# Row means of tiles 10 to 15: by two GpSimd transfers each through a row in memory instead of a TensorE transpose

## What is computed

```python
xn = _layernorm(x, axis=-1)                      # (x - mean) * rstd, per row
q = xn @ Wq.T + bq                               # every 4th head of 32 is used: 8 heads x 128
sig_q = elu(q) + 1
retrieved = (sig_q @ M) / (sig_q . z + 1e-6)     # per head
attention = repeat(retrieved, 4 heads) @ Wo.T
dense = xn @ (w * w_scale) + b
out = x + attention + dense
```

## Time and profile before

| | us |
|---|---|
| median of 3 runs | 237.94 |
| the runs | 237.94, 237.75, 238.29 |
| the profiled execution, its own time | 237.95 |
| its span, first to last instruction | 236.1 |
| TensorE busy in it | 232.5 |
| VectorE busy | 174.0 |
| ScalarE busy | 125.2 |
| GpSimd busy | 107.4 |

### The profile page before, as it was taken

The page is one execution under the profiler, slowest core; times in us unless marked ns, Lnnn a source line. Parts: engine busy times, 40 slices in busy tenths (PEclk is TensorE's granted clock), DMA queues, the critical chain, the costliest instruction groups (busy, mean ns, idle before and its releaser), DMA issues.

```text
span 236.1 us, 3421 instructions
## 1 busy us (share of the span) xinstructions
PE 232.5 (98%) x1037; PEld 188.4 (80%) x1037; DVE 174.0 (74%) x275; ACT 125.2 (53%) x285; POOL 107.4 (45%) x117
## 2 busy tenths in 40 slices
PE   8999999999999999999999999999999999999995
PEld 3688788888888788888888888888888888888895
DVE  2989999897589987997858859585667879362511
ACT  4845358687298386585547253654637445630300
POOL 1029437856932356558350442524045598480000
PEclk9999999999999999999999999999999999999999
DMA  6999999999590144471727272431134456879521
GB/s 227 389 412 414 356 250 254 224 212 218 133 278 17 41 95 130 96 180 48 175 89 178 72 196 77 91 104 39 52 94 97 136 135 159 191 189 182 193 98 44
DMA packets 24081, 38.76 MB, mean 164 GB/s; under 512 B 5440, under 2 KB 13248, under 8 KB 22912
## 3 DMA queue, kind: packets, MB, share of 16 engines
q1 hardware_dynamic: 18816, 26.10, 33.7%
q0 software_dynamic: 3808, 11.14, 24.5%
q10 hardware_dynamic: 1440, 1.31, 1.9%
HBM read 25.95 MB, written 4.19 MB: 128 GB/s over the span
## 4 chain that ended last, share of the span: by engine, by line
PE 98%; DVE 0%; issue 0%
PE attn_ps L876 14%; PE attn_ps L878 14%; PE attn_ps L877 13%; PE q_ps L876 10%; PE q_ps L878 10%; PE q_ps L877 10%; PE dense_ps L876 6%; PE dense_ps L878 6%; PE dense_ps L877 6%; PE dense_ps L967 2%; PE q_ps L916 1%; PE q_ps L904 1%; PE q_ps L911 1%; PE attn_ps L916 1%; PE attn_ps L904 1%; PE attn_ps L911 1%
## 5 line engine op out<-in xcount | busy, mean ns | idle before, releaser
L489 ACT ACTIVATE s<-s,rden 128x128 f32<-128x128 f32 x128 | 39.2, 390 | 39.3 <-DVE rden L707 37.6
L341 POOL TENSOR_TENSOR e_and_sz<-s,z_b 128x512 f32<-128x512 f32 x32 | 41.7, 1340 | 39.6 <-DVE den L703 39.6
L876 PE MATMUL attn_ps<-P_hi,aT_hi 128*128 128x512 f32 (+1 forms) x136 | 53.0, 389 | 0.0
L878 PE MATMUL attn_ps<-P_hi,aT_lo 128*128 128x512 f32 (+1 forms) x136 | 52.2, 384 | 0.0
L877 PE MATMUL attn_ps<-P_lo,aT_hi 128*128 128x512 f32 (+1 forms) x136 | 52.1, 383 | 0.0
L876 PE MATMUL q_ps<-WqT_hi,xT_hi 128*128 128x512 f32 x104 | 40.7, 391 | 0.0
L878 PE MATMUL q_ps<-WqT_hi,xT_lo 128*128 128x512 f32 x104 | 40.5, 389 | 0.0
L877 PE MATMUL q_ps<-WqT_lo,xT_hi 128*128 128x512 f32 x104 | 40.5, 389 | 0.0
L691 DVE SCALAR_TENSOR_TENSOR q_ps<-q_ps,rstd,bq_b 128x512 f32<-128x512 f32 x28 | 21.0, 752 | 17.6 <-PE q_ps L878 17.6
L876 PEld LDWEIGHTS attn_ps<-P_hi,aT_hi 128*128 128x128 f32 x136 | 25.6, 188 | 6.1 <-issue 0.6
L878 PEld LDWEIGHTS attn_ps<-P_hi,aT_lo 128*128 128x128 f32 x136 | 25.6, 188 | 5.2
(11 more groups left out here) (96 smaller groups left out, 356.1 us busy)
## 6 DMA issues: line engine op xcount, KB each, us to landing
x<-in_WoT POOLq DMA_DIRECT2D x6, 1024.0 KB, 11.0
x<-in_b POOLq DMA_DIRECT2D x16, 256.0 KB, 4.4
out<-x SPq DMA_DIRECT2D x15, 256.0 KB, 2.4
x<-in_x SPq DMA_DIRECT2D x14, 256.0 KB, 3.6
xT<-in_xT SPq DMA_DIRECT2D x13, 256.0 KB, 3.8
aT<-s SPq DMA_DIRECT2D x104, 32.0 KB, 2.3
MT<-s SPq DMA_DIRECT2D x72, 32.0 KB, 1.9
x<-in_WoT SPq DMA_DIRECT2D x2, 1024.0 KB, 13.3
```

The lines of the kernel that those rows point to most:

```text
L341: nc.gpsimd.tensor_tensor(sz_eps[:, :, h * D // 2:(h + 1) * D // 2].rearrange("p g (j c) -> p j g c", j=2), by_quarter(sbuf_s[:, t % SRING ...
L489: last = nc.scalar.activation(a_g, a_g, ACT.Copy, scale=rden[:, t % 2, g:g + 1])
L876: nc.tensor.matmul(out, x_hi, w_hi, start=start, stop=False)
L878: return nc.tensor.matmul(out, x_lo, w_hi, start=False, stop=stop)
```

## The change

Means of tiles 2 to 9 stay with TensorE. For tiles 10 to 15 the transpose (L886) and the copy from its bank (L430) are gone, six of each. In their place GpSimd issues two transfers per tile. `send_mean(t)` writes the column of 128 means, 4 bytes from each partition, to row t of a table in memory, once VectorE has them. `bring_mean(t)` waits until that has landed, and reads the row back to all 128 partitions (512 bytes each) into `mean_b`. `center(t)` waits for this second landing in place of ScalarE's copy. It stands one step later than before: tile t + 1 in step t, behind the first tile of `times_z`, where it was tile t + 2 at the end of step t.

```diff
--- before.py
+++ after.py
@@ -35,6 +35,7 @@
     XRING = 4
     HRING = 4
     BEHIND = 3
+    FIRST_CARRIED = 10
     assert P == D and HID == 512 and HALF == 512 and R == 4 and T == 16 and G == 8 and K == 4
 
     with ExitStack() as ctx:
@@ -77,6 +78,8 @@
         warm = sb("warm", [P, P], BF16)
         table_loaded = sb("table_loaded", [P, 1])
 
+        means_d = nc.dram_tensor("means", (T, P), F32, kind="Internal").ap()
+
         w_words = aT[:, 0:2, :].rearrange("p a (k w) -> p (a k) w", k=K // 2).bitcast(I32)
         w_i8 = w_words.bitcast(I8)
         WqT_raw = sbuf_s[:, 0:K, :]
@@ -125,6 +128,8 @@
         rstd_ready = sem("rstd_ready")
         mean_filled = sem("mean_filled")
         mean_copied = sem("mean_copied")
+        mean_sent = sem("mean_sent")
+        mean_brought = sem("mean_brought")
         xc_by_dve = sem("xc_by_dve")
         xc_by_pool = sem("xc_by_pool")
         xT_hi_ready = sem("xT_hi_ready")
@@ -310,8 +315,20 @@
                 nc.gpsimd.tensor_tensor(rstd[:, t:t + 1], vareps[:, t:t + 1], neg_half[:], ALU.pow
                                         ).then_inc(rstd_ready, 1)
 
+            def send_mean(t):
+                pool.wait_ge(meanvar_ready, moments_before(t) + 1)
+                nc.gpsimd.dma_start(means_d[t].rearrange("(p c) -> p c", c=1), meanvar[:, t, 0:1]).then_inc(mean_sent, 16)
+
+            def bring_mean(t):
+                pool.wait_ge(mean_sent, 16 * (t - FIRST_CARRIED + 1))
+                pool.wait_ge(xc_by_pool, t - 4)
+                nc.gpsimd.dma_start(mean_b[:, t % 2, :], means_d[t].unsqueeze(0).to_broadcast([P, P])).then_inc(mean_brought, 16)
+
             def center(t):
-                pool.wait_ge(mean_copied, t - 2)
+                if t < FIRST_CARRIED:
+                    pool.wait_ge(mean_copied, t - 2)
+                else:
+                    pool.wait_ge(mean_brought, 16 * (t - FIRST_CARRIED + 1))
                 pool.wait_ge(xT_in[6 if t == 7 else t], 16)
                 nc.gpsimd.tensor_tensor(xT[:, t % XRING, :, :], xT[:, t % XRING, :, :],
                                         mean_b[:, t % 2, :].unsqueeze(1).to_broadcast([P, K, P]), ALU.subtract
@@ -403,16 +420,23 @@
             times_z(4, 0)
             times_z(4, 1)
             for t in range(LEAD, T):
+                if FIRST_CARRIED <= t + 1 < T:
+                    bring_mean(t + 1)
                 if t > LEAD:
                     for u in denominators_of_step(t):
                         if u == T - 2:
                             spread_last_group(FIRST_SHARED + 1)
                         times_z(u, 0)
                         times_z(u, 1)
+                        if FIRST_CARRIED <= t + 1 < T and u == denominators_of_step(t)[0]:
+                            center(t + 1)
+                if FIRST_CARRIED <= t + 2 < T:
+                    send_mean(t + 2)
                 add_b(t - LEAD + 1)
                 if t + 2 < T:
                     rstd_of(t + 2)
-                    center(t + 2)
+                    if t + 2 < FIRST_CARRIED:
+                        center(t + 2)
             times_z(T - 1, 0)
             times_z(T - 1, 1)
             for t in range(FIRST_SHARED + 2, T):
@@ -583,7 +607,7 @@
                     copy_xT_hi(t + 2)
                 if t >= LAG:
                     copy_aT_hi(t - LAG + 1)
-                if LEAD < t < T - 2:
+                if LEAD < t < FIRST_CARRIED - 2:
                     copy_mean(t + 2)
                 if t >= T - 2:
                     spread_group(FIRST_SHARED + t - T + 2)
@@ -1048,7 +1072,7 @@
                 product_dense(t)
                 if t == LEAD:
                     product_P(6)
-                if t + 2 < T:
+                if t + 2 < FIRST_CARRIED:
                     spread_mean(t + 2)
                 if t == LEAD:
                     product_P(7)
```

## The result

| | before | changed |
|---|---|---|
| median of 6 runs, us | 237.95 | 255.1 |
| lowest and highest | 237.75, 238.29 | 253.55, 258.29 |
| the profiled execution | 237.95 | 258.29 |
| its span | 236.1 | 256.1 |

The ratio is 1.0713, with a 95% interval of 1.0692 to 1.0734: the change makes the kernel slower by 17 us. The forecast was 237.05. The profiled execution of the changed kernel is the slowest of its six, 3 us above the median, so its rows show somewhat more of the loss than the median has.

The account below looks back on a forecast made before the run. TensorE, busy 98% of the span, was taken as the bound, with nothing late for it. Six transposes at 0.15 us save 0.90 and all else is hidden: 237.95 - 0.90 = 237.05 us, range 236.85 to 237.3, chance 78%.

Parts of the forecast that it names:

- TensorE's term: Six transposes leave TensorE in steps 8 to 13, 0.15 us each by the difference of two steps: 0.90 us saved.
- The duration of 271 ns: Rival C, 3%: on TensorE each transpose costs its full 271 ns, giving 236.3 us.
- The signs named for it: On TensorE: steps 8 to 13 take 13.60 us, transpose group has 8 instructions, no wait over 0.3 us beyond start-up.
- the landing of the write: GpSimd's write of means lands in 2.5 us, range 2.1 to 7.5; hidden, so no cost.
- rival B: 5%: the round trip becomes the bound from 10.1 us per landing on; at 10.6, 243 us.
- rival A: 14%: nothing measurable; places save only 0.72 us, and late landings in tight steps or the end return 0.4: 237.6 us.
- The tight case: Tile 11, steps 8 and 9 dense on GpSimd: centring ends at 112.2, just in time for ScalarE; 5.0 us cover behind.
- the issues: GpSimd's two new transfer issues per tile take 0.9 us each.
- `add_b` and `rstd_of` behind the write: On GpSimd they come about 3 and 2 us later, but are needed only two steps on: no cost.
- ScalarE's copies: Six copies of 0.26 us leave ScalarE, which is busy 53% and off the path: worth nothing.
- its sign: Sign of rival B (5%): GpSimd waits for its own transfers longer than for VectorE.
- the wait of q on xT_lo in step 10: Sign that the forecast is wrong: TensorE's q waits on xT_lo in step 10 or 11, pointing to rival A or B.

Follow-up runs that it names:

- without the transfers: Changed kernel minus its twelve transfers and the waits on them; centring of tiles 10 to 15 subtracts the row left in the buffer: 236.96 us, ratio 0.9958.
- unused write: Kernel before, transposes kept, plus the six writes of means to memory that nothing reads: 248.22 and 238.03 us; then 12 executions, median 238.11.
- quarter row: Changed kernel writing only the first 32 means, side by side in memory, with the read from the row of b: 240.96 and 237.37 us.
- the version with both transfers through SBUF: Changed kernel with the means written to a row in one SBUF partition and read from there to all 128: 238.75 us, ratio 1.0045.
- the long clean chain: Changed kernel with five awaited writes in a row, pieces 512 bytes apart, before a read from the row of b: 263.17 us, ratio 1.1051.
- the two versions with three transfers per tile: Changed kernel with column to SBUF row, row to memory, memory to all partitions: all by GpSimd 236.89 us; second and third by ScalarE 236.98 us.
- the four runs that had two transfers with a clean write: Changed kernel with write to SBUF row (237.46 us), to memory 512 (237.44) or 64 bytes apart (237.41), or both transfers through SBUF (238.75).
- the write not awaited: Changed kernel with the write into one row kept, but the read takes the row of b without waiting for it: 244.83 us median.

## Why the prediction was wrong

**TensorE's term was right.** Six times 0.15 us from the difference of two steps gave 0.90 and 237.05; without the transfers the kernel takes 236.96, 0.94 under the kernel before. The duration of 271 ns, and 1.6 us with it, would have been wrong, as argued. The signs named for it (13.60 us per step, eight transposes) are there where the operand is in time.

**The first step that failed: the landing of the write.** The text took 2.5 us, "since it is tiny", between 2.1 and 7.5 from the nearest rows. It took 8.2 in the median and 7.3 to 10.0: outside both ends. What made it unlike the nearest rows is not its size. 128 pieces of 4 bytes that are 64 or 512 bytes apart land in 1.8 and 1.9 us, and side by side in an SBUF row in 2.1. Only side by side in memory they take 8.2. The text said of the pieces that "no row prices it", and still put an upper end of rows that have no such pieces. The Trainium skill's rule that was quoted, read-modify-write below 512 bytes ("DMA: Bandwidth & Descriptors", Specifications), pointed to this transfer. It gives no price, and the size of the pieces alone does not make one here, since the same pieces are cheap when they lie apart. Whether the rule is behind the slow neighbours, no run here shows. The Trainium skill's fixed cost of about 2.0 us per DMA of GpSimd ("DMA: Bandwidth & Descriptors", Anatomy of one DMA) agrees with the 1.8 to 2.1 us of the clean writes.

**The second: the point from which the round trip decides.** The text reckoned for rival B from the moment when VectorE has the mean (153.1) to the moment when TensorE wants the tile, and found 20.2 us for the two landings, 10.1 for each. But in GpSimd's program the write for tile t + 2 stands behind the centring of tile t + 1, and the read for t + 2 behind that write. So the centring cannot start a round earlier than the last one ended: write, read and centring form a loop, once per tile, and it must fit into a step. The limit is 13.6 - 1.3 = 12.3 us for both landings, 6.1 each, not 10.1. The measured 8.2 + 5.8 = 14.0 lie between the two limits: no cost by the text's rule, a loop of 15.3 us and more by the right one. The same slip is in rival A, where two landings of 7.5 cost 0.4 us. They make a loop of 16.3 us, longer than the 15.3 of the measured medians, which went with a loss of 17 us. So with the loop written down, the text's own upper ends would have given a loss of that size and not 0.4 us. (Rival A also counts the read's 7.5 from the end of its issue, where the profile counts from the start: 0.9 us too late, so that its 0.4 would be nothing.)

The tight case has a gap of its own: it lets `center(10)` run right behind `times_z(6)` and never asks whether tile 10's read has landed. Its write went out at 92.51, and the two landings of 9.3 and 4.8 us put the centring at 107.01, not at 101.6.

From write to write in the profiled execution, the rounds are 14.9 to 16.7 us. q(15) starts at 189.45, where it starts at 174.94 without the transfers, although step 9 starts at nearly the same place in both (93.1 and 93.3): 14.5 us. Tile 10's own trip makes q(10) 2.8 us later (109.71 against 106.94); the other 11.7 come in the five rounds behind it.

**The third: what the new transfer does to others was not asked.** The text costed the transfers in their queue and on GpSimd, and took the landings of all others as given. The unused write shows that up to 10 us can come from this alone. In the changed kernel the six `add_b` behind the writes land in 7.3 to 11.9 us, not in 4.4 (the median of all sixteen, 5.8, hides it), and the read in 5.8 and not in 3.2 to 3.5. The read goes out only when the write has landed, so it is not the write itself that it stands behind. Nor is it the row that it reads, since in the run with the quarter row it reads the row of b and takes 4.7. In the last four rounds the held-up `add_b` is still under way when it is issued (148.35 against a landing at 151.7 in the round shown), but in the first two hardly, and it takes 4.8 and 6.0 there. What makes it late stays open.

**The clock was left out.** The wait of 2.7 us ahead of q(15) costs about 1.6 us more behind it: one distance of 0.59 us and six of 0.43, where 0.23 is usual. The spans with and without the transfers differ by 20.9 us (256.1 and 235.2). TensorE's waits for q's and attention's operands are 10.2 + 3.1 = 13.3 of it, and its busy time is 238.9 against 231.5, 7.4 more: overlap is counted once, so most of this is the time at the lower clock.

**Right in the text:** the issues cost GpSimd little (0.6 us each, not 0.9); `add_b` and `rstd_of` behind the write did no harm; ScalarE's copies were worth nothing; the landing of the write was named as the place of rival B, and its sign (GpSimd waits longer for its own transfers than for VectorE: 56.4 us against 22.0) was the one that came, and so was the wait of q on xT_lo in step 10 (2.83 us). Its chance, 5%, rested on the first two wrong steps.

## What to carry to other kernels

Before pricing a new transfer by leads, write down the loop that it closes on the engine that issues and awaits it: everything between two turns of the same instruction has to fit into one step, whatever lead the data has. Do not write a column of single numbers side by side into memory: collect it in one partition of SBUF first, and store it from there in one piece (2.1 + 2.8 us, against 8.2 and other transfers held up). Take the price of a small operation on a full engine from the difference of two steps with and without it, which was right here to 0.1 us.

## What the runs showed of the hardware that was not expected

- 128 pieces of 4 bytes written to memory: 8.2 us side by side, 1.8 at 64 bytes apart, 1.9 at 512 bytes apart; 32 side by side 5.0. To an SBUF row side by side: 2.1 (2.6 in the version with both transfers through SBUF).
- While such a write is under way, a read of another row from the same queue landed in 11.2 us instead of 3.5, 256 KB with an addition in 7.3 to 11.9 instead of 4.4, and blocks of SyncE in up to 11.0 us (2.3 in the median and 7.8 at most in the kernel before). Whether that reaches the end varies from run to run: eight of 12 executions at 238 to 240 us, four at 244 to 247.
- A transpose among matmuls of 512 columns takes 0.15 us of TensorE's time with a duration of 0.27.
- The time around the span was 1.8 us in the kernel before, without transfers, with the unused write, with the long clean chain, and in the two versions with three transfers per tile. It was 2.2 to 2.3 in the changed kernel, in the quarter row, and in the four runs that had two transfers with a clean write, and 1.9 to 2.0 with the write not awaited. What sets it stays open.
